# Second cross-attention: weighted sums in visits of four chunks, six slots for exponentials, one set of sums

## What is computed

```python
# q: (16, 64, 256) normed latents; k, v: (16, 1601, 256) the context
qn, kn, vn = layernorm(q), layernorm(k), layernorm(v)
Q = (qn @ Wq + bq).reshape(b, l, 16, 16)
K = (kn @ Wk + bk).reshape(b, s, 16, 16)
V = (vn @ Wv + bv).reshape(b, s, 16, 16)
A = softmax(0.25 * einsum('blhe,bshe->bhls', Q, K), axis=-1)
O = einsum('bhls,bshd->blhd', A, V) + Q
out = transpose(O, (0, 2, 1, 3)).reshape(b, l, 256)
return layernorm(out) @ Wo + bo + out
```

## Time and profile before

| | |
|---|---|
| median of three runs | 1474.97 us (1474.6 to 1480.98) |
| the profiled execution | 1468.6 us, span 1466.8 us |
| mean granted TensorE clock | 0.953 of full speed |
| busy: PE, DVE, ACT, POOL | 1341.1, 998.1, 646.5, 691.3 us |
| the second cross-attention | about 405 to 1255 us of the span |

### The profile page before, as it was taken

One profiled execution on the slowest core, in us unless ns is written; L12 is line 12 of the kernel. 1 busy time (PEld: TensorE's weight loads), 2 busy tenths in 40 slices (PEclk: granted clock), 3 DMA queues, 4 the chain that ended last, 5 costly groups with the idle time before them and its releaser, 6 DMA issues. The chain is left out here.

```text
span 1466.8 us, 29125 instructions
## 1 busy us (share of the span) xinstructions
PE 1341.1 (91%) x11170; PEld 1088.4 (74%) x11170; DVE 998.1 (68%) x2019; ACT 646.5 (44%) x1230; POOL 691.3 (47%) x592
## 2 busy tenths in 40 slices
PE   7899768589978999999999999999999998699998
PEld 4556455479957888888888888888888877467787
DVE  6998653545656777877787778777767666454444
ACT  3556213310164655565555555555555533243322
POOL 0142002120244777977797678667866645131100
PEclk9999889789989999999999999999999987899999
DMA  9998126007256777877787778777866470220000
GB/s 361 422 380 314 73 102 230 1 0 244 75 137 182 193 186 194 234 198 182 195 234 197 181 196 238 190 172 202 219 156 146 98 165 24 79 115 0 1 0 29
DMA packets 107575, 240.11 MB, mean 164 GB/s; under 512 B 30218, under 2 KB 76634, under 8 KB 104746
## 3 DMA queue, kind: packets, MB, share of 16 engines
q1 hardware_dynamic: 89070, 216.75, 52.0%
q10 hardware_dynamic: 18368, 21.50, 4.3%
HBM read 152.96 MB, written 6.40 MB: 109 GB/s over the span
## 5 line engine op out<-in xcount | busy, mean ns | idle before, releaser
L2458 DVE TENSOR_REDUCE d_top<-psum 128x1 f32<-128x400 f32 (+2 forms) x512 | 285.5, 573 | 81.0 <-PE psum L2007 72.6
L1898 POOL TENSOR_TENSOR d_ring<-d_ring 128x512 f32<-128x512 f32 x224 | 289.5, 1292 | 68.5 <-ACT d_ring L2246 50.4
L2246 ACT ACTIVATE d_ring<-psum 128x512 f32<-128x512 f32 (+1 forms) x416 | 229.8, 595 | 170.1 <-PE psum L2025 127.7
L2025 PEld LDWEIGHTS psum<-d_queries,d_stack 100*128 100x128 f32 (+1 forms) x1664 | 209.9, 192 | 40.8 <-issue 25.7
L2025 PE MATMUL psum<-d_queries,d_stack 100*128 100x128 f32 (+1 forms) x1664 | 229.1, 279 | 9.2 <-DVE d_queries L2473 6.0
L2007 PE MATMUL psum<-d_stack,d_queries 96*128 96x400 f32 (+1 forms) x512 | 203.1, 400 | 6.4 <-DVE d_top L2458 4.9
L1991 PE MATMUL psum<-d_wv,d_rowsT 128*128 128x256 f32 (+1 forms) x1248 | 206.8, 283 | 0.0
L1991 PEld LDWEIGHTS psum<-d_wv,d_rowsT 128*128 128x128 f32 (+1 forms) x1248 | 192.7, 186 | 1.9 <-issue 0.5
L1835 POOL TENSOR_TENSOR d_rowsT<-shared,d_rowsT 128x768 fp32r<-128x768 f32 (+2 forms) x62 | 118.6, 1915 | 149.2 <-ACT d_rowsT L2217 149.2
L1981 PE MATMUL psum<-d_rowsT,d_wk 128*128 128x384 f32 (+2 forms) x768 | 158.5, 355 | 11.8 <-DVE d_bv L2618 7.3
L1981 PEld LDWEIGHTS psum<-d_rowsT,d_wk 128*128 128x128 f32 x768 | 132.9, 192 | 23.3 <-DVE d_bv L2618 7.4
(11 more groups left out here) (419 smaller groups left out, 2153.8 us busy)
## 6 DMA issues: line engine op xcount, KB each, us to landing
d_stack<-d_stage SPq DMA_DIRECT2D x384, 200.2 KB, 4.3
a_cT<-ctxT_dram SPq DMA_DIRECT2D x14, 1601.0 KB, 13.8
a_cR<-ctx_rows_dram ACTq DMA_DIRECT2D x12, 1664.0 KB, 11.0
shared<-moe_w_dram SPq DMA_DIRECT2D x16, 1024.0 KB, 10.2
shared<-row_stds_dram SPq DMA_DIRECT2D x16, 801.0 KB, 6.5
shared<-ctxT_dram SPq DMA_DIRECT2D x32, 384.0 KB, 6.8
shared<-ctx_rows_dram SPq DMA_DIRECT2D x12, 896.0 KB, 5.9
shared<-ctx_rows_dram SPq DMA_DIRECT2D x12, 768.0 KB, 5.6
```

The costliest lines, as they stand in the source:

```text
L1898: pool.tensor_tensor(sums[:, 0, m, :], first, ring[:, slot_of(u, m, c), :], ALU.add)\
L2025: last = pe.matmul(ps[0:w, S_BANK + (m + c) % 2, j * P:(j + 1) * P], stack[0:STACKED, m, j, c * P:c * P + w], queries[0:STACKED, m, j, :], ...
L2246: act.activation(ring[0:w, slot_of(u, m, c), :], ps[0:w, S_BANK + (m + c) % 2, :], ACT.Exp)\
L2458: dve.tensor_reduce(top[:, m, v:v + 1], ps[:, M_BANK + v % 2, 0:min(w, S - s0)], X, ALU.max)\
```

## The change

`weigh` is called in steps 2, 4 and 6 for four chunks each (`WEIGH_AT`) in place of two chunks in each of steps 1 to 6; chunk 12 stays in step 0 of the next quad. The ring has eight places as before: six now hold exponentials (`SLOTS`), in place of four, and two hold the sums, one of POOL's and one of DVE's, in place of two each. An exponential therefore waits for what was done with chunk c - 6. As one set of sums serves every quad, the first add of a quad waits for `denominators` of the quad just before (`d_den_ps` against `n`, not `n - 1`), and DVE's first add, chunk 1, stands in step 1 behind the lows and `take_heads`, not at the end of step 0. The diff, cut to its core:

```diff
+    SLOTS = 6
+    WEIGH_AT = {2: (0, 1, 2, 3), 4: (4, 5, 6, 7), 6: (8, 9, 10, 11)}
...
-        sums = ring[:, 4:8, :].rearrange("p (e u) n -> p e u n", e=2)
+        sums = ring[:, SLOTS:SLOTS + 2, :]
...
-        def slot_of(u, m, c):
-
-            return (2 * u + m + c) % 4
+        def slot_of(b, m, c):
+
+            return (NC * (2 * b + m) + c) % SLOTS
...
 # POOL, add
                 if c == 3:
-                    wait(pool, "d_den_ps", n - 1)
-                    first = ring[:, slot_of(u, m, 2), :]
+                    wait(pool, "d_den_ps", n)
+                    first = ring[:, slot_of(b, m, 2), :]
...
 # PE, batch
-                        if g:
-                            for c in GROUPS[g - 1]:
-                                weigh(b, u, m, c)
-                        elif m or not first:
+                        for c in WEIGH_AT.get(g, ()):
+                            weigh(b, u, m, c)
+                        if g == 0 and (m or not first):
                             weigh(*before(b, u, m), NC - 1)
...
 # ACT, exp
-                wait(act, "d_weigh_ps", NC * n + c - 3)
-                n0, c0 = (n, c - 4) if c >= 4 else (n - 1, NC + c - 4)
+                wait(act, "d_weigh_ps", NC * n + c - SLOTS + 1)
+                n0, c0 = (n, c - SLOTS) if c >= SLOTS else (n - 1, NC + c - SLOTS)
...
 # DVE, add
                 if c == 1:
-                    wait(dve, "d_den_ps", n - 1)
-                    first = ring[0:w, slot_of(u, m, 0), :]
+                    wait(dve, "d_den_ps", n)
+                    first = ring[0:w, slot_of(b, m, 0), :]
...
 # DVE, batch
-                        for c in (1,) if g == 0 else GROUPS[g - 1]:
-                            if c in VECTOR_ADDS and (g == 0 or c > 1):
+                        for c in GROUPS[g - 1] if g else ():
+                            if c in VECTOR_ADDS:
                                 add(b, u, m, c)
```

## The result

| | before | after |
|---|---|---|
| median | 1476.2 us (1474.6 to 1480.98) | 1646.26 us (1634.53 to 1652.01) |
| profiled execution, span | 1468.6, 1466.8 us | 1645.88, 1644.0 us |
| mean granted TensorE clock | 0.953 | 0.889 |
| busy: PE, DVE, ACT, POOL | 1341.1, 998.1, 646.5, 691.3 us | 1420.1, 1058.8, 646.0, 693.0 us |

The ratio is 1.114 (interval 1.110 to 1.118): slower, by 170 us where I forecast 97, and 38 us above the top of my range.

What follows compares the result with a forecast made beforehand. A quad's path was taken to run PE, ACT, DVE's chain to take 0, then PE and DVE alternating. Quad delays of 65 us plus 32 for the clock gave 97 on 1468.6, 1566; forecast 1570 us, range 1528 to 1608.

Steps and rivals of the forecast that it cites:

- merged visits and six slots: Fewer `weigh` visits on PE cost 0.56 us a quad; six exponential slots save 0.33 us per even quad.
- held adds: DVE's add of chunk 1, moved to step 1, waits out POOL: 2.45 us per odd quad, 1.2 per even.
- clock: PE's clock falls to half after stands ahead of top 2: 21 us in odd quads, 11 in even.
- Part 1, the visits: PE's visits go from seven to four a quad, yet lie less well against DVE's waits: +0.56 us a quad.
- part 3, the stall of exponential 12: Six slots free score 1 of even quads from waiting for exponential 12: -0.33 us per even quad.
- Part 2, odd quads: Step 1: POOL's low rows of quarter 0 hold the add of chunk 1, delaying take 0 by 2.45 us.
- Part 2, even quads: Step 1: the add meets POOL's scalings or sums; 1.2 us taken, bounds 0.60 and 2.6.
- Part 4, the clock: PE's stands ahead of top 2 bring 3.4 us at half clock, 1.5 us lost each; 32 us in all.
- (a): Rival: the add is held but PE's clock stays at its upper level: 1540 us, chance 0.24.
- (b): Rival: DVE gets the port first, the add isn't held, 0.60 us each: 1505 us, stands of 1.5; chance 0.11.
- (c): Rival: top 2 doesn't wait for take 0, PE alone sets the pace: faster, 1453 us, chance 0.04.

Runs made afterwards that it cites:

- experiment 1: Changed kernel with DVE's add of chunk 1 back at the end of step 0; merged visits, six slots, one set of sums kept: 1479.18 us, ratio 1.0027.
- experiment 6: Changed kernel plus 13, 12 and 6 unread matmuls ahead of odd top 2, `denominators` behind an odd quad, and even top 2: 1576.74 us, ratio 1.0697.
- experiment 3: Changed kernel with POOL's low rows of quarters 0 and 1 moved to step 3 of odd quads: 1540.06 and 1564.26 us in two runs.
- experiment 2: Kernel before with only DVE's add of chunk 1 moved from step 0 to step 1; visits, slots, sums as before: 1613.68 us, ratio 1.0946.
- experiment 4: Changed kernel with POOL's low rows (odd quads) and scalings (even quads) of quarters 0 and 1 moved to step 3: 1527.59 us, ratio 1.0363.
- experiment 7: Kernel of experiment 1 with visits re-placed: two chunks in step 1, four each in 3 and 5, two in 6: 1460.13 us, ratio 0.990.

## Why the prediction was wrong

The direction held, and the add of chunk 1 was the right place to look; the size was not right, because a second place was missing. Term by term, what I had put down against what the runs measured:

| term | forecast | measured | by |
|---|---|---|---|
| merged visits and six slots | 12 us (31 x 0.56 less 15 x 0.33) | 4 us | experiment 1 |
| held adds | 53 us (the rest of the 65) | 99 us | experiment 6 less 1 |
| clock | 32 us | 65 us | after less experiment 6 |
| sum | 97 us | 168 us (170 by the medians) | |

- **Part 1, the visits, and part 3, the stall of exponential 12: right in kind, a little high.** Experiment 1's 4 us are 0.13 us a quad where the sum had 0.56 - 0.33 / 2 = 0.4. Which of its terms was too high no run shows.
- **Part 2, odd quads: right.** 2.45 us of delay forecast; take 0 starts at 925.81, 2.40 after the place at 923.41 that the add now fills. The add takes 2.47, begins behind POOL by the 0.43 us that the earlier trace rows gave, and ends 0.55 after it. The Trainium skill (SBUF — State Buffer, Who interferes with whom) has a DVE instruction with two SBUF inputs fully blocked by a GpSimd instruction that reads SBUF; the 2.47 us here and the 0.68 of experiment 3 agree, and by a shared bandwidth the add would have taken some 1.2.
- **Part 2, even quads: about right.** 1.2 us taken, with ends at 0.60 and 2.6; the twelve even adds between 480 and 1200 us take 0.68 to 1.79, 1.5 in the mean. The one at 956.38 takes 1.79, held by POOL's sums, and PE stands 1.59 ahead of top 2, against the 2.05 that I had put there.
- **The step that failed stands in part 3.** I wrote that POOL is delayed 0.55 by each add "and then waits less, because the quad is longer". A longer quad does the opposite. POOL's work per quad is the same, so in a longer quad it catches up with ACT: its wait for exponentials goes from 8.9 to 118.6 us, and what doesn't hang on exponentials, the low rows of quarter 3 and the scalings, starts 4.3 us earlier against DVE. It lands on the adds of chunks 10 to 12, which in the kernel before met only the end of POOL's last sum and short instructions: 5.80 us in place of 2.74. I had costed only the instruction that moved, and taken the others from the trace of before at their old neighbours. The term that was missing: 5.80 - 2.74 = 3.1 us, and a stand of 2.83 us ahead of `denominators`, in each of the 12 waits listed; 14 times some 3 us are 42, an estimate, of the 46 us by which the held adds exceed the forecast. That the moved add alone sets POOL ahead, experiments 1 and 2 show (a wait of 1.6 us without the move, 116.8 with it); that the longer quad is how, is read from the traces, since no run lengthens the quad by other means.
- **Part 4, the clock: right in kind, half the size.** I had one stretch of 3.4 us at 0.50 behind each odd stand and half as many behind the even ones, 5.1 us a batch. The rows show 6.82 us behind the odd stand (927.98 to 934.80), 3.41 behind the stand of `denominators` that I had not seen, and 3.40 behind the even one of 1.59 us: 13.6 us in this batch. By the stage's clock it is 132 us in 550, or 14.7 a batch of 61.45. The price of each was not too low: 65 us over 14 batches are 4.6 us for 14.7, a third of the time at the lower level, where I took 1.5 of 3.4. There were nearly three times as many. The upper bound that I gave, two stretches in a row after each, is what the odd quad above shows, and the range took in only a part of it.
- **The rivals.** (a), the clock staying up, put at 1540, is nearest to experiment 6 with 1577: too low by the same missing stand. (b), the add not held, put at 1505 with stands of 1.5 us, is nearest to experiment 4, 1528 with stands of 1.36 and 1.6; the rest of that difference I have not taken apart, its stage is at 0.95 of the clock. (c) fell: top 2 does wait for take 0.

Open is why the same stand is followed by a lower clock in one quad and not in another (below). And the split into 99 and 65 us rests on one way of keeping PE busy.

## What to carry to other kernels

An instruction moved on an engine that another can hold, as POOL holds DVE's adds here, is priced by what runs beside it in its new place; and if it lengthens the period, every other pair of the two engines has to be looked at again, since the engine with slack moves forward against the others and meets what it never met before. Work that looks like overhead on the busiest engine may lie in a wait of it: merge or drop it only where the timeline shows that what follows it starts late because of it, as experiment 7 does, and leave it where the engine would stand without it. Count the stands that a change makes before the clock behind them is priced: here each held add made one of its own, and the clock took as much again as two thirds of what they cost.

## What the runs showed of the hardware

**Who comes first decides, and the loser may be POOL.** In the kernel before, DVE's three adds start at 750.70 and POOL's 128 by 128 multiplication at 751.23 takes 0.87 us; after, the same one at 941.54, with no add beside it, takes 0.42. The Trainium skill (SBUF — State Buffer, Who interferes with whom) says "Issue order, not op shape, decides who blocks." Both rows agree, and so does the case: where DVE's adds come first, POOL loses half a microsecond; where POOL's low rows and scalings come first, the adds lose three.

**The length of a stand alone doesn't tell what the clock does.** I had reasoned from stands of 1.25 us, not followed by a lower clock, and of 2.29, followed by one. In experiment 4 the two stands of 1.36 us shown above, at the same place of two quads, are followed by these stretches:

```profile
920.36:923.76 3.40, 3.40 (x48) 2.98 (x49) 2.41 (x5) 0.60 (x1) 3.26 (x3) 1.00 0.92 187
974.12:977.52 3.40, 3.40 (x25) 2.99 (x29) 2.06 (x4) 0.60 (x1) 3.26 (x3) 0.50 1.02 204
```

2.4 GHz behind the first, 1.2 GHz behind the second, with half as many matmuls done (25 against 48). Of the thirteen odd stands of 1.36 us in that run between 540 and 1190 us, six are followed by the lower level and seven are not. In the kernel after, and in experiment 2, all stands of 2.39 us and more between 480 and 1230 us go with time at the lower level. In these runs a stand of 1.36 to 1.62 us has to be counted as a maybe.
